# A graph transformer on one core: the mixer in column tiles and in another order, and a new start of the first graph

## The reference

```python
x = x + L0_gnn(layernorm(x), adj)     # 8 graphs of 1024 nodes, 128 features
x = x + L0_ffn(layernorm(x), ...)     # shared expert and two of eight routed experts
x = x + L1_gnn(layernorm(x), adj)     # four heads of sigmoid attention on the edges
x = x + L1_ffn(layernorm(x), ...)     # tokens into 64 slices per head, a mixer over them, and back
...
# L0_gnn
norm = (sum(adj, -1) + 1e-6) ** -0.5
f_hom = adj @ ((x @ theta) * norm) * norm
gate = sigmoid(x @ W_t + b_t); out = elu(gate * f_hom + (1 - gate) * (x @ W_h))
...
# the mixer, on st: 8 graphs x 64 slices x 512 channels, 8 heads of 64
z, xBC, dt = split(st @ in_w.T)                # 512, 512 + 64 + 64, 8 forward + 8 backward
dt = softplus(dt + dt_bias)
x, Bm, Cm = split(silu(causal_conv3(xBC)))
dA = exp(-dt * exp(A_log))
y = scan over the 64 slices, forward and backward: h = h * dA + dt * Bm * x; y = h . Cm
y = y + x * repeat(x @ fcD_w.T + D, 64)        # the skip
yg = y * silu(z)
yg = yg * rsqrt(mean(yg ** 2) + 1e-5) * norm_w
return yg @ out_w.T
```

## Time and profile before

| | us |
|---|---|
| median of three runs | 1431.44 |
| lowest, highest | 1429.69, 1431.56 |
| the profiled execution, its own time | 1430.97 |
| its span, from the first to the last instruction | 1429.2 |
| TensorE busy, matmul records | 1348.6 |
| VectorE, ScalarE, GpSimd busy | 970.7, 792.0, 570.9 |
| mean granted TensorE clock | 0.99 |

### The profile page before, as it was taken

One profiled execution on the slowest core, in us unless ns is written; L12 is line 12 of the kernel. 1 busy time (PEld: TensorE's weight loads), 2 busy tenths in 40 slices (PEclk: granted clock), 3 DMA queues, 4 the chain that ended last, 5 costly groups with the idle time before them and its releaser, 6 DMA issues. The chain is left out here.

```text
span 1429.2 us, 27447 instructions
## 1 busy us (share of the span) xinstructions
PE 1348.6 (94%) x10127; PEld 808.1 (57%) x10127; DVE 970.7 (68%) x2153; ACT 792.0 (55%) x1327; POOL 570.9 (40%) x496
## 2 busy tenths in 40 slices
PE   4999999999999999986899999999998889999998
PEld 1455555668999999752233233333232567764498
DVE  2467887633333333457989999999995999948633
ACT  2466655643444444436677787777773768854100
POOL 2027776762555555301202323222151789951000
PEclk9999999999999999999999999999999999999999
DMA  9757747355888878554434533423422402004034
GB/s 313 269 177 265 284 153 231 116 183 153 251 244 247 251 242 248 170 169 153 137 99 132 163 97 119 126 90 105 129 80 59 132 15 60 1 10 87 1 106 133
DMA packets 199832, 214.37 MB, mean 150 GB/s; under 512 B 22677, under 2 KB 156309, under 8 KB 199700
## 3 DMA queue, kind: packets, MB, share of 16 engines
q1 hardware_dynamic: 191284, 195.24, 44.4%
q0 software_dynamic: 8416, 17.38, 3.4%
HBM read 170.51 MB, written 42.06 MB: 149 GB/s over the span
## 5 line engine op out<-in xcount | busy, mean ns | idle before, releaser
L1541 ACT ACTIVATE c_AH<-c_S 128x2048 f32<-128x2048 f32 x128 | 240.7, 1881 | 130.1 <-PE c_S L1406 129.8
L1575 DVE TENSOR_TENSOR c_AH<-c_AH,c_A 128x2048 f32<-128x2048 f32 x128 | 292.1, 2286 | 24.1 <-ACT c_AH L1541 20.6
L866 ACT ACTIVATE a_A<-a_DG,a_A 128x256 f32<-128x256 f32 (+2 forms) x202 | 94.8, 509 | 193.4 <-PE a_DG L724 192.2
L617 POOL DMA_INDIRECT ys<-a_A,a_targets x135 | 131.2, 972 | 143.6 <-DVE a_A L1079 125.1
L1364 POOL TENSOR_TENSOR c_raw<-c_deg,c_power 128x16 f32<-128x16 f32 x16 | 58.2, 3636 | 243.1 <-DVE c_deg L1632 243.1
L591 POOL DMA_INDIRECT rows<-a_S,a_slots x128 | 132.2, 1032 | 51.6 <-issue 51.3
L1433 PE MATMUL c_DG<-c_AH,c_ones 128*32 128x512 f32 x1024 | 137.3, 608 | 8.6 <-DVE c_AH L1575 8.6
L1406 PE MATMUL c_S<-c_Q,c_K 32*128 32x512 f32 x928 | 132.4, 640 | 5.1 <-ACT c_AH L1541 3.1
L1419 PE MATMUL c_YA<-c_AH,c_XT 128*32 128x512 f32 x1024 | 131.9, 593 | 0.3 <-DVE c_XT L1642 0.3
L694 PE MATMUL a_AG<-a_A,x 128*128 128x512 f32 x256 | 114.5, 596 | 0.0
L724 PE MATMUL a_DG<-a_A 128*128 128x256 f32 (+2 forms) x356 | 99.4, 403 | 1.9 <-DMA a_A<-xT_all 1.8
(11 more groups left out here) (414 smaller groups left out, 2506.6 us busy)
## 6 DMA issues: line engine op xcount, KB each, us to landing
a_A<-in_dram SPq DMA_DIRECT2D x76, 578.0 KB, 5.1
a_A<-in_dram SPq DMA_DIRECT2D x32, 1024.0 KB, 10.0
c_A<-in_dram SPq DMA_DIRECT2D x128, 256.0 KB, 2.6
a_A<-rows SPq DMA_DIRECT2D x60, 130.0 KB
G<-ys SPq DMA_DIRECT2D x10, 512.0 KB, 5.1
a_X<-in_dram SPq DMA_DIRECT2D x8, 512.0 KB, 12.8
a_R<-in_dram SPq DMA_DIRECT2D x8, 512.0 KB, 4.8
stream<-a_R SPq DMA_DIRECT2D x8, 512.0 KB, 10.1
```

The lines of the kernel that those rows point to most:

```text
L617: pool.indirect_dma_start(ys, bass.IndirectOffsetOnAxis(ap=targets[g % NY][:, t:t + 1], axis=0), Y[g % NY][:, t, :], None, bounds_check=ys ...
L866: act.activation(hT[g % 2][:, f, 0:size(g)], up_bank(g, f)[:, 0:size(g)], ACT.Gelu, bias=w_of(g)[:, F_N + f:F_N + f + 1]).then_inc(h_ready, 1)
L1541: act.activation(AH[g % UNITS][:, :, :], S[:, :, :], ACT.Sigmoid, scale=HD ** -0.5).then_inc(att_ready, 1)
L1575: dve.tensor_tensor(ah[:, :, :], ah[:, :, :], A[g % ADJ_BUFS][:, :].unsqueeze(1).to_broadcast([P, HEADS, HALF]), ALU.mult).then_inc(ah_dve, 1)
```

## The change

At the front: twenty transposes of the identity, once `shift1` is raised, then the first graph's `x_transposes`, and only then its degrees. ScalarE's `copy_xnT(0)` moves ahead of `copy_dpart(0)`. In the mixer: dt is projected in four column groups of 32 (each with 128 of the columns), so that it and its softplus lie on 128 partitions x 128 columns; X2 and X3 and `G_` come ahead of Z; the skip's factor is first computed per head (`HEADS_`, four products in column groups) and then expanded to channels by a 0/1 matrix that GpSimd makes; ScalarE adds D, and GpSimd multiplies with X after the mix; the forward half of the product with `G_` goes to GpSimd; the sum of squares uses 32 columns of ones in column groups and four small products in place of VectorE's masked sum.

```diff
@@ front_stage, TensorE
-                pe.wait_ge(deg_ready, i + 1)
+                if i > 0:
+                    pe.wait_ge(deg_ready, i + 1)
...
                 if i >= 2:
                     pe.wait_ge(dif_ready, i - 1)
                 elif i == 1:
+                    pe.wait_ge(deg_ready, 1)
+                else:
                     pe.wait_ge(xnT_ready, NH)
...
             pe.wait_ge(consts, 2)
+            pe.wait_ge(shift1, 1)
+            for _ in range(WARM):
+                pe.transpose(AG[:, 0:P], ident[:, :], ident[:, :])
+            x_transposes(0)
             degrees(0)
             degree_transposes(0)
...
@@ hydra_stage, SyncE
-            sp.dma_start(dA_rows, dA).then_inc(dA_stored, 16)
-            sp.wait_ge(dA_stored, 16)
+            for c in range(BP):
+                sp.dma_start(dA_rows[:, c * P:(c + 1) * P], dA[(c + 1) * LANE - DTS:(c + 1) * LANE, :]).then_inc(dA_stored, 16)
+            sp.wait_ge(dA_stored, 16 * BP)
@@ GpSimd
             pool.wait_ge(later, 32)
+            pool.wait_ge(dts_ready, 1)
             pool.tensor_tensor(outw[:, :, :], outw[:, :, :], nw[:, :].unsqueeze(2).to_broadcast([P, KT, INNER]),
                                ALU.mult).then_inc(outw_ready, 1)
+            pool.wait_ge(x_psum, KT)
+            pool.memset(expand, 0.0).then_inc(wide_ready, 1)
+            for c in range(KT):
+                pool.wait_ge(wide_ready, 3 + c)
+                pool.affine_select(out=expand, in_=expand, compare_op=ALU.not_equal, fill=1.0, base=-c * LANE,
+                                   pattern=[[-1, SH], [0, SP_]], channel_multiplier=1).then_inc(wide_ready, 1)
             pool.wait_ge(decay_loaded, 32)
             pool.memset(decay[:, 0:SH, :, 0:1], 0.0).then_inc(ends_ready, 1)
...
-            pool.wait_ge(z_psum, KT)
+            pool.wait_ge(gs_ready, 1)
+            pool.wait_ge(fw_ready, 1)
+            fw = decay[:, 0:SH, :, :]
+            pool.tensor_tensor(fw, fw, gs[:, :].rearrange("p (b l) -> p b l", b=BP).unsqueeze(1).to_broadcast(
+                [P, SH, BP, G_N]), ALU.mult).then_inc(fw_ready, 1)
+            pool.wait_ge(mix_ready, 1)
             for k in range(KT):
...
+                pool.wait_ge(scale_ready, k + 1)
+                pool.tensor_tensor(XC[:, k, :], scale_of[:, k, :], XC[:, k, :], ALU.mult).then_inc(skip_ready, 1)
@@ TensorE
-            project(DT_[0:DTS, :], in_x, INNER + 2 * NS, DTS, dt_psum)
+            for k in range(KT):
+                for c in range(BP):
+                    mm = pe.matmul(DT_[c * LANE:(c + 1) * LANE, 0:P], in_x[:, k, REST - LANE:REST], st[:, k, c * P:(c + 1) * P],
+                                   start=(k == 0), stop=(k == KT - 1))
+            mm.then_inc(dt_psum, 1)
...
+            for c in range(KT):
+                mm = pe.matmul(HEADS_[c * LANE:(c + 1) * LANE, :], fcD_wide[:, c, :], XC[:, c, :], start=True, stop=True)
+            mm.then_inc(heads_psum, 1)
+            pe.wait_ge(heads_ready, 1)
             for k in range(KT):
                 pe.wait_ge(z_ready, k + 1)
-                pe.wait_ge(skip_w, k + 1)
-                for c in range(KT):
-                    mm = pe.matmul(Z_[k][:, :], skipw[:, k, c, :], XC[:, c, :], start=(c == 0), stop=(c == KT - 1))
-                mm.then_inc(fcd_psum, 1)
+                pe.matmul(Z_[k][:, :], expand[:, 2 * k:2 * k + 2, :].rearrange("p h d -> p (h d)"), by_head,
+                          start=True, stop=True).then_inc(fcd_psum, 1)
...
                 pe.wait_ge(squared, k + 1)
-                mm = pe.matmul(SUM_[:, :], ones[:, :], Z[k], start=(k == 0), stop=(k == KT - 1))
+                for c in range(BP):
+                    mm = pe.matmul(SUM_[c * LANE:(c + 1) * LANE, 0:P], ones[:, :], Z[k][:, c * P:(c + 1) * P],
+                                   start=(k == 0), stop=(k == KT - 1))
...
             for j in range(KT):
+                if j == 2:
+                    sum_transposes()
                 out_part(j, KT - 1)
@@ ScalarE
             act.activation(dA, dts, ACT.Exp, scale=A[:, :]).then_inc(dA_ready, 1)
+            act.wait_ge(bc_conv, 1)
+            act.activation(TH[1][:, :], BC[:, :], ACT.Tanh).then_inc(bc_tanh, 1)
             for k in range(1, KT):
                 tap(XC[:, k, :], X_[k][:, :], k, x_psum, k + 1)
-            act.wait_ge(bc_conv, 1)
-            act.activation(TH[1][:, :], BC[:, :], ACT.Tanh).then_inc(bc_tanh, 1)
@@ VectorE
             for k in range(KT):
                 dve.wait_ge(first_tap, k + 2)
                 convolve(XC[:, k, :], X_[k][:, :], cw[:, k, :], x_conv)
-            dve.wait_ge(bc_tanh, 1)
-            gate(BC[0:NS, :], BC[0:NS, :], TH[1][0:NS, :], bc_ready)
-            gate(Cm[:, :], BC[NS:2 * NS, :], TH[1][NS:2 * NS, :], bc_ready)
-            for k in range(KT):
-                dve.wait_ge(x_tanh, k + 1)
-                gate(XC[:, k, :], XC[:, k, :], TH[k % 2][:, :], x_ready)
+                if k == 0:
+                    dve.wait_ge(bc_tanh, 1)
+                    gate(BC[0:NS, :], BC[0:NS, :], TH[1][0:NS, :], bc_ready)
+                    gate(Cm[:, :], BC[NS:2 * NS, :], TH[1][NS:2 * NS, :], bc_ready)
+                else:
+                    gate_x(k - 1)
             dve.wait_ge(dttok_psum, 1)
+            dve.wait_ge(x_psum, KT)
             spread(0)
+            gate_x(KT - 1)
+            dve.wait_ge(source_read, 1)
+            dve.wait_ge(ends_ready, 2)
+            dve.tensor_tensor_scan(M[:, 0:half], M[:, 0:half], source, 0.0, ALU.mult, ALU.add).then_inc(fw_ready, 1)
+            dve.wait_ge(fw_ready, 1)
+            spread(SH)
             gate_z(0)
             gate_z(1)
...
-            dve.wait_ge(fcd_psum, KT)
-            for k in range(KT):
-                dve.scalar_tensor_tensor(out=XC[:, k, :], in0=Z_[k][:, :], scalar=Dc[:, k:k + 1], in1=XC[:, k, :],
-                                         op0=ALU.add, op1=ALU.mult).then_inc(skip_ready, 1)
```

More of the change, by code:

```diff
@@ L29 @@
 FIRST = 2
+WARM = 20
 TO_ADD = {1: T, 2: T, 3: T, 4: T, 5: T}
@@ L2180, in hydra_stage @@
         foldw = Wc[:, :].rearrange("p (k d) -> p k d", k=KT)
-        power, ones = sb("power", [P, B]), sb("ones", [P, P])
+        power, ones = sb("power", [P, B]), sb("ones", [P, LANE])
         diag = sb("diag", [P, G_N])
@@ L2190, in hydra_stage @@
         half = SH * BP * G_N
-        tmp = [M[0:DTS, k * ROWS_ALL:(k + 1) * ROWS_ALL] for k in range(6)]
+        tmp = [M[:, k * P:(k + 1) * P] for k in range(6)]
         dA = tmp[5]
-        dts = Z[KT - 1][0:DTS, :]
+        dts = Z[KT - 1][:, 0:P]
         by_row = lambda a: a.rearrange("p (j b l) -> p j b l", b=BP, l=G_N)
@@ L2198, in hydra_stage @@
         OT = inz[:, :].rearrange("p (k r) -> p k r", k=KT)
-        skipw = inz[:, :].rearrange("p (k c d) -> p k c d", k=KT, c=KT)
+        scale_of = inz[:, :].rearrange("p (k r) -> p k r", k=KT)
+        fcD_wide = sb("fcD_wide", [P, KT, LANE])
+        expand = inx[:, half:half + INNER].rearrange("p (h d) -> p h d", h=SH)
+        by_head = scale_of[:, KT - 1, :]
+        gs, sq = sb("gs", [P, BP * G_N]), sb("sq", [P, P])
         xtok = ST[:, :, :, :].rearrange("p k b g -> p (k b g)").rearrange("p (b c) -> p b c", b=BP)
@@ L2293, in _ @@
             mm.then_inc(g_psum, 1)
+            pe.wait_ge(z_loaded, 16 * KT)
+            for k in range(KT):
+                if k >= 2:
+                    pe.wait_ge(x_conv, k - 1)
+                project(Z_[k][:, :], in_z, k * P, P, z_psum)
+            pe.wait_ge(x_conv, KT)
+            pe.wait_ge(gs_ready, 1)
             pe.wait_ge(x_ready, KT)
@@ L2330, in sum_part, with sum_transposes @@
                 pe.wait_ge(squared, k + 1)
-                mm = pe.matmul(SUM_[:, :], ones[:, :], Z[k], start=(k == 0), stop=(k == KT - 1))
+                for c in range(BP):
+                    mm = pe.matmul(SUM_[c * LANE:(c + 1) * LANE, 0:P], ones[:, :], Z[k][:, c * P:(c + 1) * P],
+                                   start=(k == 0), stop=(k == KT - 1))
                 if k == KT - 1:
                     mm.then_inc(sum_psum, 1)
+            def sum_transposes():
+                by_lane = ident[:, :].rearrange("p (c z) -> p c z", z=LANE)[:, :, 0]
+                pe.wait_ge(sq_ready, 1)
+                for q in range(2):
+                    for s in range(2):
+                        mm = pe.matmul(SUM_[s * G_N:(s + 1) * G_N, P + q * BP:P + (q + 1) * BP], sq[:, q * G_N:(q + 1) * G_N], by_lane,
+                                       start=True, stop=True)
+                mm.then_inc(sumT_psum, 1)
             pe.wait_ge(outw_ready, 1)
@@ L2402, in _ @@
                 act.activation(xtok[:, b, :], XTOK_[b % 2][:, :], ACT.Copy).then_inc(xtok_ready, 1)
+            act.wait_ge(heads_psum, 1)
+            act.activation(by_head, HEADS_[:, :], ACT.Copy).then_inc(heads_ready, 1)
+            for k in range(KT):
+                act.wait_ge(fcd_psum, k + 1)
```

(4 more changed lines are left out.)

83 lines of the change are left out of this document (44 added, 39 removed).

## The result

| | median, us | range, us | runs |
|---|---|---|---|
| before, same chip | 1430.57 | 1426.41 to 1431.56 | 6 |
| after | 1420.24 | 1416.52 to 1422.78 | 6 |
| after, profiled execution (span 1418.2) | 1419.9 | | 1 |

The ratio is 0.993, with an interval of 0.9917 to 0.9944: 8 to 12 us faster. On a second chip the same pair gave 0.9941 (0.9924 to 0.9958), 8.6 us between the medians 1429.43 and 1420.85. In both profiled executions 1.7 to 1.8 us lie between the span and the execution's own time, not the 1.5 given ahead of the prediction.

What follows compares the result with a forecast made beforehand. TensorE, busy 94% of the span, was taken as the bound, with VectorE near it in the mixer. Front -0.2 and mixer -5.5 made -5.7 us, forecast 1425.8 us, range 1423.0 to 1429.6.

Steps and rivals of the forecast that it cites:

- front term: Front: degrees at full clock gain 2.26 us, half clock behind the longer gap costs 2.1; together -0.2 us.
- the gates beside GpSimd: Mixer after y: the first two VectorE gates each wait for GpSimd's multiplications, together 1.1 us.
- the 0.8 for the expanding products: Mixer: clock falls in a 3.8 us TensorE gap; four expanding matmuls take up to 6.9 instead of 3.44, +0.8 us.
- Rival 1: Front: transposes don't raise the clock, degrees stay at half clock and the gap still loses it; +2.7, 1428.5 us; 10%.
- Rival 2: Front: the gap behind the transform keeps its clock, or it comes back fast; -2, 1423.8 us; 15%.
- a gap of 1.7 to 1.9 kept its clock: Front before the change: TensorE's idle gap from 29.7 to 31.4 was taken not to lower the clock.
- Rival 4: Mixer: GpSimd's four selections become the new wait; at 3.7 us each the gain is cancelled, over 4.4 slower; 4%.
- Rival 5: Mixer: column tiles don't run side by side, dt and the sum stay at 3.44 each; +4.8, 1430.6 us; 4%.
- The sum of squares: Mixer: 8 records of 3.44 us become 32 packed and eight small ones, plus changes of form; -1.5 us.
- the four changes of form: Mixer, sum of squares: four switches of matmul form at 0.1 us each, together 0.4; up to 0.5 each as upper end.
- rival 3: Mixer: the clock falls at y and the output projections start at half clock; +3, 1428.8 us; 12%.

Runs made afterwards that it cites:

- the tanh experiment: Whole changed kernel, with ScalarE's tanhs put between the convolution taps instead of after all of them: 1421.14 us, ratio 0.9932 to the kernel before.
- the filled front: Whole changed kernel plus forty more identity transposes in TensorE's gap between the first graph's eight transform products: 1419.0 us, ratio 0.992 to the kernel before.

## Why the prediction was right and wrong

The change gained 8.6 to 10.3 us where 5.7 was forecast. The mechanisms of the sum held. Its front term rested on an old gap that "kept its clock" and loses it half the time; two of its mixer terms, the gates beside GpSimd and the 0.8 for the expanding products, were too dear; and the stretch between front and mixer, put at nothing, was 4.8 us shorter in the first pair of profiles and 0.9 in the second.

**The front, right in its mechanism.** The transposes were done at 14.66 (forecast 15.2), the input's at 15.53, the degrees took 3.64, the gap was 4.59 (4.3), the clock fell, and the eight products behind it paid 1.37 + 1.23 = 2.6 us in that profile (forecast 2.1). The second degrees came at 41.3; by the forecast's -0.2 it would have been 40.9. Rival 1 falls with the kernel without the transposes. Rival 2 has two halves: the 4.6 us gap lost the clock in all eight profiles in which it was left open, but the clock came back sooner in two of them (2.83 + 1.91 and 2.92 + 1.55 us for the eight products), and those have the earliest second degrees, 40.32 and 39.98 (their adjacency also landed 0.1 to 0.2 us before that of the first profile).

**The front, wrong in its baseline.** One step that failed is "a gap of 1.7 to 1.9 kept its clock", and with it the use of one profile as the price of before. The four profiles of the old front put the second degrees at 41.12, 40.91, 43.21 and 43.47, mean 42.2. The seven of the new one without filler have 41.29, 41.35, 41.53, 41.65, 41.93, 40.32 and 39.98, mean 41.15. That is -1.0, not -0.2, and the front alone measured -1.3. Besides the gap, the old degrees themselves took 5.71 to 6.39 us, where the forecast had 5.90 for all.

**The mixer up to y, right in its sum, partly by luck.** The mix and its copies ended at 46.8 after the start (forecast 47.2), dt's group took 1.08, VectorE waited 3.61 for the first tanh (4.4 forecast), and the decay was not last. But two misses cancel: the first scan started at 27.4, not 28.6, since gates, convolutions and spread took less than I had added up, and the backward scan took 1.1 us longer than any term allowed, behind GpSimd's product. Rival 4 falls: the four selections took 3.85 together, 0.96 each where I took 0.9, and the decay's DMA landed after them. The decay was near, though: its end memsets were over 1.2 us ahead of the scan, and in the tanh experiment they were the bound. Rival 5 falls with dt's 1.08 and with 0.64 + 0.62 for the sums.

**The gates, the term that was mis-sized.** I took a wait of 1.1 us for the first two gates together, from a tiny operation that ended with GpSimd's in the earlier trace rows. That mechanism holds: VectorE waits for the end of GpSimd's present multiplication. What a gate pays is therefore only what is left of that one when the gate starts. In the second profile of the changed kernel that was 0.07 and 0.42 us, and the gates were longer by 0 and 0.29; in the first profile they were longer by 0.10 and 0.29. TensorE's continuous stretch began at 51.71, not 52.8: -5.9 instead of -4.8. Of these 1.1 us, 0.4 is y's earlier start and 0.7 the gates: from y's start to the stretch it was 4.9, not 5.6. (The prediction has two prices for that wait, 1.1 and, were it absent, 1.7; 4.9 with 0.3 of waiting in it fits the 1.1.) Up to y the same turns cost more than I had counted: two gates of B and C took 3.54 us instead of the 1.4 of two such gates before (GpSimd's product on the output weights ended at 1292.43), and the backward scan 5.55 instead of 4.42. The first lies ahead of VectorE's wait for tanh and is covered by it.

**The sum of squares, right.** In the first profile the column groups took 1.01 us (1341.42 to 1342.43) and the small products 0.33 (1344.34 to 1344.67), for 3.43 before: 2.1 less. From the continuous stretch's start to the folded weight's products it went from 1358.40 - 1341.14 = 17.26 to 67.27 - 51.71 = 15.56, so 1.7 less. The other 0.4 is in the projections around them; it is the size that I had put on the four changes of form, but no run tests that they are its cause.

**The clock in the mixer, a term that wasn't there.** I charged 0.8 for the expanding products at 1.2 GHz, behind a gap of 3.8 us. The gap was 2.56 in the first profile, and the 8 records took 3.7 to 4.2 us in every profile of the new mixer but one. In the kernel without the twenty transposes they did take 6.21 us, and the stage was 67.28 all the same: the mix covers them. What does cost is y at 1.2 GHz, rival 3's fall, in the changed kernel's first profile and in the filled front's: 68.43 and 68.41 instead of 67.3, 1.1 us, not 3. I put that down to the holes which TensorE at full speed has there (0.49 ahead of 1334.13 in the second profile) and which the slower work fills. The tanh experiment shows the same trade: y came 1.1 earlier, was slow, and the stage was 67.33. So the stage is 6.4 or 7.6 shorter, not 5.5. The 2.1 us between 7.6 and 5.5 are the 0.8 of the expanding products, 0.7 of the gates, 0.4 of y's start and 0.2 of the sum of squares.

**The stretch between, put at nothing.** The forecast has no term for the 1240 us between the front and the mixer. In the first pair of profiles that is the largest part of the miss: -11.0 instead of -5.7 is +0.4 from the front, -0.9 from the mixer and -4.8 from this stretch. In the second pair -8.1 instead of -5.7 is +0.6, -2.1 and -0.9. What makes the stretch differ stays open, see below.

**What is left.** -1.0 to -1.3 and -6.4 to -7.6 make -7.4 to -8.9, and the second chip's -8.6 lies there. The first chip's -10.3 has an interval of -8 to -12. The baseline from which I forecast, three runs with a median of 1431.44, was high: with three more runs on that chip it became 1430.57, and the same kernel beside the experiments has medians of 1430.77, 1429.43 and 1427.94. One sum of the prediction does not come out: half of rival 1 and a third of rival 3 make the chance of faster 0.79, not 0.76. And the unchanged stretch differs from one execution to the next. Its length in the changed kernel's two profiles (length, busy times, granted clock, DMA share, GB/s):

```profile
41.29:1278.92 1237.63, 1187.75 (x9092) 698.78 (x9092) 885.18 (x2017) 755.33 (x1261) 554.38 (x464) 0.99 0.49 153
```

```profile
41.35:1282.42 1241.07, 1190.60 (x9092) 700.78 (x9092) 885.59 (x2017) 755.68 (x1261) 555.52 (x464) 0.99 0.49 152
```

It is the same 9092 records, 2.85 us more of TensorE's busy time in the second, and 3.4 us of length. The difference lies in three places behind 1100 us, behind idle times of TensorE of 4.44, 2.25 and 0.69 us, the same in both executions. The first profile has

```profile
1106.42 1.04 PE L102 MATMUL s_TP<-ident,carry 128*128 128x128 f32 x8
...
1165.45 1.06 PE L102 MATMUL s_TP<-ident,x 128*128 128x128 f32 x8 [2.25 <-issue]
...
1274.32 1.94 PE L1945 MATMUL s_TP<-M,ST 128*64 128x512 f32 x8 [0.69 <-ACT M L1990]
```

and the second

```profile
1106.67 1.91 PE L102 MATMUL s_TP<-ident,carry 128*128 128x128 f32 x8
...
1166.82 1.69 PE L102 MATMUL s_TP<-ident,x 128*128 128x128 f32 x8 [2.26 <-issue]
...
1276.12 3.52 PE L1945 MATMUL s_TP<-M,ST 128*64 128x512 f32 x8 [0.69 <-ACT M L1990]
```

In the first the granted clock is 1.00 in all three rows, in the second 0.50, 0.59 and 0.53.

**Still open.** Over all profiles that stretch took 1241.0 to 1242.4 us behind the four old fronts and 1241.2 behind the one without the twenty transposes, but 1235.9 to 1239.1 behind eight of the nine new fronts with them. Most of this is one step and not scatter. From the end of the 4.44 us gap to the mixer's start it is 179.0 to 179.3 us in six profiles (the five without the twenty transposes, and the second one of the changed kernel) and 175.7 to 176.0 in the other eight, with nothing between. The two small loads fewer are not what decides it: the kernel with the front alone still has them and is on the short course, the one with the mixer alone lacks them and is on the long one. The split would say that the new front also shifts which later gaps lose the clock, by some 3.3 us in its favour. The timed runs don't bear it out: the front alone gained 1.3 us, with 0.3 lost to 2.9 gained as its bounds, and three of the twelve timed runs of the repeated kernel before lay at 1425.6 to 1426.7 too. One profile per kernel can't settle it, no run was made for it alone, and what puts an execution on the one course or the other is not shown.

## What to carry to other kernels

Where an edit only fills or opens idle time of TensorE, price it against several profiles of the kernel before: a gap of 1.88 us kept the clock in two executions and lost it in two, which is 1.7 us, more than the edit was worth. Look behind the edit as well: the same code some 1060 us later ran in one of two courses, 3.3 us apart. Waking the clock while a load was still under way cost nothing here, but what is won must not end in a longer gap; the order of work behind it has to be filled too. In a stage that VectorE bounds, look for what is second last before removing a wait: taking away a wait of 3.6 us brought y 1.1 forward, and 3.1 once the decay's source was moved too. And where GpSimd takes over work of VectorE, ask at what moment each of its instructions ends, since VectorE pays the rest of the one it meets.

## What the runs showed of the hardware

- Fp32 transposes of 128x128 alone, twenty in one profile and twenty-eight in another, brought TensorE from 1.2 to 2.4 GHz: the degrees took 3.64 us behind them and 6.30 without the first twenty.
- The clock also fell behind shorter gaps, and not each time: one of 1.88 us lost it in two profiles of four, one of 2.25 us (at 1165) in six of fourteen.
- VectorE and GpSimd take turns by whole instructions where VectorE reads two operands from SBUF. Three of VectorE's rows lose what was left of GpSimd's instruction but for 0.13 to 0.15 us: 2.15 us of 2.28 left (two gates, 3.54 for 1.39), 1.13 of 1.26 (the backward scan, beside a product that began at 1310.86 and took 4.55), 0.94 of 1.09 (the mix, with GpSimd's multiplications ahead of it). GpSimd waits in the same way: 3.31 and 3.24 for 1.27. A copy with one SBUF operand waited too (1.25 for 0.19); the spread, with one operand in PSUM, did not (2.29 beside GpSimd's product of 4.55, 2.28 without).
- The same kernel, the one before, took 1425.4 to 1432.6 us in 24 runs on one chip, and its profiles differ in which gaps lose the clock. That these falls make the whole scatter was not tested.
